# Attend pass of a Performer and RWKV block: where TensorE takes the maxima of a group, and where VectorE reduces them

## The reference

```
def _phi(u, omega):                       # 16 heads of 32, 128 features
    proj = einsum('bhsk,mk->bhsm', u, omega)
    sq   = 0.5 * sum(u * u, axis=-1, keepdims=True)
    stab = max(proj, axis=-1, keepdims=True)
    return exp(proj - sq - stab) / sqrt(128) + 1e-06

pq, pk = _phi(q * scale, omega), _phi(k * scale, omega)
kv, z  = einsum('bhsm,bhsk->bhmk', pk, v), sum(pk, axis=2)
num    = einsum('bhsm,bhmk->bhsk', pq, kv)
den    = einsum('bhsm,bhm->bhs', pq, z)
h      = (num / den) @ wo
y      = layernorm(xn + h)                # then feed-forward, gelu, a second layernorm

r   = sigmoid(xr @ W_r.T)                 # xr, xk: mixes of xn and xn of the token before
out = r * (square(relu(xk @ W_k.T)) @ W_v.T)
```

## Time and profile before

| | |
|---|---|
| median of 3 runs | 3194.19 us (3192.41 to 3194.93) |
| the profiled execution | 3190.72 us, span 3188.9 us |
| PE, weight loads | 3125.2 us (98%), 2770.3 us (87%) |
| DVE, ACT, POOL | 72%, 52%, 32% of the span |
| keys pass, attend pass, feed-forward pass | to about 760 us, to about 1790 us, to the end |
| granted TensorE clock, mean | 0.992 |

### The profile page before, as it was taken

The page is one execution under the profiler, slowest core; times in us unless marked ns, Lnnn a source line. Parts: engine busy times, 40 slices in busy tenths (PEclk is TensorE's granted clock), DMA queues, the critical chain, the costliest instruction groups (busy, mean ns, idle before and its releaser), DMA issues.

```text
span 3188.9 us, 71767 instructions
## 1 busy us (share of the span) xinstructions
PE 3125.2 (98%) x27633; PEld 2770.3 (87%) x27633; DVE 2290.8 (72%) x4582; ACT 1644.1 (52%) x3560; POOL 1028.1 (32%) x828
## 2 busy tenths in 40 slices
PE   8999999997999999999999999999999999999998
PEld 6888888886878787777777799999999999999998
DVE  6888888886666666666666666666766766767666
ACT  5677777764555454554555544444444444444443
POOL 2455544544555565565656310000000000000000
PEclk9999999998999999999999999999999999999999
DMA  7666666654354544444444665444445554444454
GB/s 227 202 188 194 201 187 200 197 189 101 90 156 115 144 126 131 125 134 123 138 135 117 201 218 171 157 163 158 152 161 166 167 171 159 160 165 148 160 169 133
DMA packets 450307, 510.17 MB, mean 160 GB/s; under 512 B 298800, under 2 KB 323888, under 8 KB 449968
## 3 DMA queue, kind: packets, MB, share of 16 engines
q1 hardware_dynamic: 449968, 505.59, 51.0%
HBM read 342.83 MB, written 162.66 MB: 159 GB/s over the span
## 4 chain that ended last, share of the span: by engine, by line
PE 55%; POOL 10%; DVE 3%; issue 3%; ACT 3%; DMA 2%; SPq 1%; ACTq 0%; DVEq 0%; POOLq 0%
PE ffn_hidden L188 29%; PE shared_bank L188 12%; PE ffn_result L188 7%; POOL shared_y L1209 3%; PE attend_feat L1372 2%; POOL shared_y L1207 2%; POOL attend_oT_lo L1191 2%; PE attend_num L1410 2%; PE attend_turn L1410 2%; POOL attend_ka_lo L1187 1%; POOL shared_mix_lo L1183 1%; DMA ffn_r_in<-r_d 1%; DVE ffn_yb L1834 1%; ACT attend_act_k L1252 1%; ACT attend_ka_hi L1256 1%
## 5 line engine op out<-in xcount | busy, mean ns | idle before, releaser
L188 PE MATMUL ffn_hidden<-ffn_yT_hi,ffn_wa_hi 128*128 128x256 f32 x2048 | 572.6, 280 | 2.5 <-DVE ffn_wa_lo L1755 2.5
L188 PE MATMUL ffn_hidden<-ffn_yT_lo,ffn_wa_hi 128*128 128x256 f32 x2048 | 573.6, 280 | 0.0
L188 PE MATMUL ffn_hidden<-ffn_yT_hi,ffn_wa_lo 128*128 128x256 f32 x2048 | 572.2, 279 | 0.0
L333 POOL TENSOR_TENSOR ffn_n_rstd<-ffn_n_base,ffn_n_power 128x2 f32<-128x2 f32 x32 | 27.5, 860 | 1274.7 <-DVE ffn_n_negmean L328 1274.7
L188 PEld LDWEIGHTS ffn_hidden<-ffn_yT_hi,ffn_wa_hi 128*128 128x128 f32 x2048 | 385.6, 188 | 3.4 <-DVE ffn_wa_lo L1755 2.7
L188 PEld LDWEIGHTS ffn_hidden<-ffn_yT_hi,ffn_wa_lo 128*128 128x128 f32 x2048 | 385.7, 188 | 0.0
L188 PEld LDWEIGHTS ffn_hidden<-ffn_yT_lo,ffn_wa_hi 128*128 128x128 f32 x2048 | 385.3, 188 | 0.2
L1737 ACT ACTIVATE ffn_ht_hi<-ffn_hs 128x512 fp32r<-128x512 f32 x248 | 156.3, 630 | 426.0 <-DVE ffn_hs L1784 426.0
L728 ACT ACTIVATE keys_e<-keys_feat,keys_below 128x128 f32<-128x128 f32 x1024 | 273.0, 436 | 187.0 <-DVE keys_below L811 187.0
L655 POOL TENSOR_TENSOR keys_z_sum<-keys_z_sum,keys_e 128x512 f32<-128x512 f32 x192 | 262.5, 1397 | 257.0 <-ACT keys_e L728 257.0
L1788 DVE TENSOR_TENSOR ffn_ht_lo<-ffn_hs,ffn_ht_hi 128x512 fp32r<-128x512 f32 x248 | 173.7, 700 | 218.7 <-ACT ffn_ht_hi L1737 218.7
(11 more groups left out here) (306 smaller groups left out, 9218.2 us busy)
## 6 DMA issues: line engine op xcount, KB each, us to landing
ffn_tq<-part_d SPq DMA_DIRECT2D x248, 512.0 KB, 5.1
keys_xin<-in_L_attn_x_dram SPq DMA_DIRECT2D x32, 512.0 KB, 4.3
xn_d<-keys_xn SPq DMA_DIRECT2D x32, 512.0 KB, 5.2
xt_d<-keys_xn_turned SPq DMA_DIRECT2D x32, 512.0 KB, 2.7
keys_xT_whole<-xt_d SPq DMA_DIRECT2D x128, 128.0 KB, 3.2
xT_d<-keys_xT_whole SPq DMA_DIRECT2D x32, 512.0 KB, 3.9
kt_d<-keys_uk_turned SPq DMA_DIRECT2D x32, 512.0 KB, 3.5
keys_kT<-kt_d SPq DMA_DIRECT2D x128, 128.0 KB, 3.4
```

The source lines that it names most:

```text
L188: last = pe.matmul(out, stationary[a], moving[b], start=start and n == 0, stop=stop and n == len(TERMS) - 1)
```

## The change

On PE, `max` 0 moves from behind the four `num` blocks to ahead of them, and `max` 1 from between `k` 0 and `k` 1 to ahead of `k` 0. A turn is then `max` 0, `num` 0 to 3, `max` 1, `k` 0, `k` 1 and the rest as it was. On DVE, `top` 0 leaves the start of the list and is done for the next group at its end, between `wo` 1 and `stats`; `HEAD` gets `top` 0 of the first group, ahead of `mix` 1. The lists of the crossing follow. No instruction is added or taken away.

```diff
--- before.py
+++ after.py
@@ -1061,12 +1061,12 @@
 
 
 
-        PE_BODY = [("num", 0, -1), ("num", 1, -1), ("num", 2, -1), ("num", 3, -1), ("max", 0, 0), ("k", 0, 0),
-                   ("max", 1, 0), ("k", 1, 0), ("r", 0, 0), ("below", 0, 0), ("feat", 0, 0), ("r", 1, 0), ("out", 0, 0),
+        PE_BODY = [("max", 0, 0), ("num", 0, -1), ("num", 1, -1), ("num", 2, -1), ("num", 3, -1), ("max", 1, 0),
+                   ("k", 0, 0), ("k", 1, 0), ("r", 0, 0), ("below", 0, 0), ("feat", 0, 0), ("r", 1, 0), ("out", 0, 0),
                    ("feat", 1, 0), ("out", 1, 0), ("wo", 0, -1), ("wo", 1, -1)]
-        DVE_BODY = [("top", 0, 0), ("top", 1, 0), ("recip", 0, -1), ("below", 0, 0), ("mix", 0, 1), ("exp", 0, 0),
+        DVE_BODY = [("top", 1, 0), ("recip", 0, -1), ("below", 0, 0), ("mix", 0, 1), ("exp", 0, 0),
                     ("o", 0, -1), ("out", 0, 0), ("turn_y", 0, -2), ("hi", 1, 0), ("out", 1, 0), ("mix", 1, 1), ("wo", 0, -1),
-                    ("wo", 1, -1), ("stats", 0, -1), ("part_lo", 0, 0)]
+                    ("wo", 1, -1), ("top", 0, 1), ("stats", 0, -1), ("part_lo", 0, 0)]
         ACT_BODY = [("num", 0, -1), ("num", 1, -1), ("num", 2, -1), ("num", 3, -1), ("norm", 0, -2), ("k", 0, 0),
                     ("k", 1, 0), ("below", 0, 0), ("kv", 0, 0), ("r", 0, 0), ("exp", 0, 0), ("mix", 0, 1), ("r", 1, 0),
                     ("oT", 0, -1), ("exp", 1, 0), ("mix", 1, 1), ("part_hi", 0, 0)]
@@ -1077,7 +1077,7 @@
                    ("rep_load", 0, -1), ("store_y", 0, -2), ("xb", 0, -1), ("store_r", 0, 0), ("store_yT", 0, -2),
                    ("kv", 0, 0),
                    ("part_load", 0, 0), ("part_store", 0, 0)]
-        HEAD = [("mix", 1)]
+        HEAD = [("top", 0), ("mix", 1)]
         OF_BATCH = {"kv": 0, "part_load": 0, "part_sums": 0, "part_hi": 1, "part_lo": 2, "part_store": 3}
 
         def run(eng, do, order):
@@ -1917,8 +1917,8 @@
         return Programs(sync, gpsimd, scalar, vector, tensor, mem), y_loaded, stored
 
 
-PE_CROSSING = (("attend", "num", 0, -2), ("attend", "num", 1, -2), ("attend", "num", 2, -2), ("attend", "num", 3, -2),
-               ("attend", "max", 0, -1), ("attend", "k", 0, -1), ("attend", "max", 1, -1), ("attend", "k", 1, -1),
+PE_CROSSING = (("attend", "max", 0, -1), ("attend", "num", 0, -2), ("attend", "num", 1, -2), ("attend", "num", 2, -2),
+               ("attend", "num", 3, -2), ("attend", "max", 1, -1), ("attend", "k", 0, -1), ("attend", "k", 1, -1),
                ("attend", "r", 0, -1), ("attend", "below", 0, -1), ("attend", "feat", 0, -1), ("attend", "r", 1, -1),
                ("attend", "out", 0, -1), ("attend", "feat", 1, -1), ("attend", "out", 1, -1), ("attend", "wo", 0, -2),
                ("attend", "wo", 1, -2), ("attend", "num", 0, -1), ("attend", "num", 1, -1), ("attend", "num", 2, -1),
@@ -1928,7 +1928,7 @@
                ("ffn", "w2", 2, 0), ("ffn", "w2", 3, 0), ("ffn", "w1", 5, 0), ("ffn", "w2", 4, 0),
                ("ffn", "w1", 6, 0), ("ffn", "w1", 7, 0), ("ffn", "w2", 5, 0),
                ("ffn", "w2", 6, 0), ("ffn", "w2", 7, 0))
-DVE_CROSSING = (("attend", "top", 0, -1), ("attend", "top", 1, -1), ("attend", "recip", 0, -2),
+DVE_CROSSING = (("attend", "top", 1, -1), ("attend", "recip", 0, -2),
                 ("attend", "below", 0, -1), ("attend", "exp", 0, -1), ("attend", "o", 0, -2),
                 ("attend", "out", 0, -1), ("attend", "turn_y", 0, -3), ("attend", "hi", 1, -1), ("attend", "out", 1, -1), ("attend", "wo", 0, -2),
                 ("ffn", "weights", 0, 0), ("attend", "wo", 1, -2), ("ffn", "turn", 0, 0), ("attend", "stats", 0, -2),
```

## The result

| | before | changed |
|---|---|---|
| median, 7 runs each | 3194.19 us (3191.12 to 3198.28) | 3204.24 us (3201.84 to 3206.89) |
| ratio to before | | 1.0031 (1.0021 to 1.0041) |
| span of the profiled execution | 3188.9 us | 3200.0 us |
| PE busy, DVE busy | 3125.2, 2290.8 us | 3121.6, 2368.4 us |

The changed kernel is 0.3% slower, 10 us. The direction and the place were as forecast (3215), but the size was not: +21 us were forecast, and +10 came. PE's busy time is hardly changed. DVE's is 78 us longer although it does the same work.

What follows compares the result with a forecast made beforehand. Two paths bound the attend pass: PE from `wo` 0 to the end of `k` 1, and POOL from the second `ka_lo` on. Terms 0 + 1 + 14 + 5 + 1 = +21 us on 3194.2 gave 3215 us, range 3195 to 3236.

Steps and rivals of the forecast that it cites:

- The statistics are 2.8 us late: On DVE in the attend pass, the statistics wait behind `top` 0 and begin 2.8 us later, delaying POOL.
- The room in turns without `part_sums`: On POOL, 3.2 us of room absorbs 2.8 in 22 groups; seven with `part_lo` lose 1 us together.
- The turn behind `part_sums`, +2.0 us: On POOL, seven groups with `part_sums` each lose 2.0 us (1.5 to 2.8), 14 us in all.
- The lateness of the second `ka_lo`: On POOL in groups with `part_sums`, the second `ka_lo` starts behind the first and ends 0.7 us later.
- The 0.1 for the small steps beside `part_sums`: DVE's three small `below` steps, now beside POOL's `part_sums`, add 0.1 us (0 to 0.3) per such group.
- the price of a `mix` piece: Each of DVE's four `mix` 0 pieces between POOL instructions costs POOL 0.3 us (0.20 to 0.42), +1.2 together.
- The clock, +5 us: PE's longer wait before `wo` dips the granted clock in 3 of 7 groups: 5 us (0 to 11).
- PE's shape changes, 0: On PE, 0.18 us saved per group is offset by `max` 0 to `num` 0: net 0 (-2 to +7).
- a period below 32.2: Sign of a wrong forecast: turns under 32.2 us would mean shape changes were dearer before than read.
- Start and crossing, +1: At the attend pass's start and crossing, delays and a shorter first wait together cost +1 us (-3 to +5).
- Rival 3: Worse: DVE's `o` waits for POOL's `mix_lo` 0 and every such group loses its clock; +41, 3235 us; chance 0.16.
- rival 1: Lateness mostly absorbed: DVE's pieces slip in for nearly nothing, the clock holds; +7, 3201 us; chance 0.24.

Runs made afterwards that it cites:

- e1: The changed kernel with DVE's statistics put ahead of the next group's first maxima again, PE's new order kept: 3202.17 us, 1.0023 of before.
- e2: The changed kernel with PE's part undone and DVE's part kept, so the statistics wait for later maxima: 3321.25 us, 1.0400 of before.
- e3: The changed kernel with POOL's `part_sums` run one turn later, behind `oT_lo`, where POOL is idle: 3192.23 us, 0.9999 of before.
- e9: The changed kernel itself measured once more, with no further edit: 3202.26 us, 1.0031 of before.
- e5: The kernel before the change with one exchange on POOL, `oT` ahead of `mix` 0: 3179.86 us, 0.9962 of before.

## Why the prediction was wrong in its size

Point by point, with the term that it used and what the runs showed:

- **The statistics are 2.8 us late: right.** POOL's root starts 5.60 us into the turn instead of 2.86. e1 takes the lateness away and the long turns go with it, e2 makes it 6.4 and both `ka_lo` start within 0.15 us of where they were worked out.
- **The room in turns without `part_sums`: right, and better than thought.** 1 us was set aside for the turns with `part_lo`; they lose nothing (32.25 against 32.23 for their neighbour).
- **The turn behind `part_sums`, +2.0 us: too dear.** Measured +1.45. PE's 0.18 has no part in it, because this turn's path doesn't pass through the `k` blocks. The lateness of the second `ka_lo` was right: it starts 15.21 into the turn on average, at 1456.2 in the turn shown, where the forecast's own steps (all times in it moved to this turn) give 1456.1. The 0.1 for the small steps beside `part_sums` was right too: from the first `part_sums` to `diff` POOL takes 3.23 us instead of 3.13. The step that failed is the price of a `mix` piece. Taken at 0.3 us between 0.20 and 0.42, it costs POOL 0.19 three times and 0.07 once: four make 0.63, not 1.2. The row of before (0.20) had shown nearly that, and I moved away from it towards a bound that no row showed. e3 shows where the term comes from: with `part_sums` moved, 1.65 us go from each of the seven turns.
- **The clock, +5 us: wrong, and the largest miss.** The granted clock didn't fall in any of the seven long turns. PE's wait rose to 1.9 us and not to 2.5, because the term above was too large. The step that failed is the comparison with the crossing. The forecast set one wait of 2.5 us against a dip, but its own rows show two waits there, 2.7 and 2.5 us, with PE busy for only 6.20 of the ten us before the dip. A long turn has one wait, and PE is busy for 8.55 of ten. In e2, where PE stands several times in a turn, the clock falls in each of the seven.
- **PE's shape changes, 0: wrong by 4 us the other way.** The loss was bounded by the opposite order, `num` to `max` with 0.41 us of idle loads, and the gain by 0.10. By the forecast's own sum the bound of 0.10 gives -0.08 in a turn. Measured is -0.18: the 0.18 that leaves the `k` blocks was read rightly, and `max` 0 ahead of `num` 0 costs nothing more. So the gain lies outside the stated -2 to +7 us. The forecast had named a period below 32.2 as a sign that it had misread the changes, and the fourth kind of turn has 32.18. By the Trainium skill's rule that a change of tiling mode drains TensorE (TensorEngine Tiling (Array Packing), section Tiling Modes) and one change fewer, the forecast had -3 us beside its own 0, and that was nearer. The equal price that this count takes for all changes isn't what the rows show: from the last matmul of one block to the first of the next, the change from column to row tiles takes 0.31 us, and those from row tiles to column tiles and to whole ones 0.21.
- **Start and crossing, +1: too cheap.** The start gave +0.5 in the profiled execution, but the second execution of the changed kernel (e9) has its second turn at 820.41, 1.2 us earlier than before, so no loss is shown there. Three of the forecast's parts can be seen: the wait for ACT's first copy shrank from 2.6 to 1.2 us, the stretch at half clock behind it (790.1 to 793.5 before) is gone, and PE waits 3.3 us for `mix_lo` where it waited 0.3, 3.0 us more, where up to 2.4 was allowed for `mix` 1 behind `top` 0. The crossing has the wait that was named there, 3.2 us and not at most 2.3, since `recip` waits for its DMA longer than it did before and `below` stands behind it. The profiled stretch is 4 to 6 us longer than before, and the wait alone costs some 4 us by the estimate above, so most of it arrives.
- **The rivals.** Rival 3's point of decision was read right: `o` came 0.15 us ahead of `mix_lo`, against 0.2 worked out, and so the worse case didn't come. The measured 3204 lies nearer to rival 1 (3201) than to the forecast: its clock, which holds, came true, and its pieces that cost nearly nothing didn't.

Sum of the terms, forecast and measured in the profiled span: PE's order 0 and -3.8; turns with `part_lo` 1 and 0 (in the line before); turns behind `part_sums` 14 and +10.2; clock 5 and 0; start and crossing 1 and +4.7. Together 21 and 11. The mechanism of the loss was right and its sizes were not: the clock and the long turns were too high, the gain in the other turns was set at nothing, and only the crossing was too low. That the crossing cost 3.7 us more than forecast is luck for the total, since it hides part of the other misses.

## What to carry to other kernels

Of a step that moves ahead of another on one engine, follow the second one's result to the engine that waits for it, and add up that engine's whole queue up to the point where the critical path enters it: room that is there in three turns of four isn't room. Price an interleaving by the row that shows it, not by a worse bound that no row shows, and give a gain its term as well as a loss. Where one engine's unbroken run ends just after the bound engine asks, look at the order within that run first: here one exchange of two POOL steps was worth more than all else.

## What the runs showed of the hardware

- Some DVE instructions and POOL's instructions take turns when both wait. DVE pays with a whole POOL instruction each time (1.67 us of work took 5.78), POOL with 0.07 to 0.19 us for a piece of 0.48 (0.40 from start to start). Those held here are `mix`, `below` and `o`, which read two SBUF tensors, and also the cast at L1312, which reads one: 1.22 us instead of 0.23. The maxima, read from PSUM, ran beside POOL at their full speed (2.49 us).
- From the last matmul of one block to the first of the next, the change from row tiles to column tiles takes as long as that from row tiles to whole ones (0.21 us), while the change from column to row tiles takes 0.31 us and leaves the weight loads idle for 0.41. A block of maxima between the two `k` blocks costs 0.18 us more than one between `wo` and `num`.
- Idle time of the weight loads of 0.55 us ahead of `wo` was worth 0.38 us of time (e5).
- A single stop of PE of 1.9 us (weight loads) was followed by full clock in seven turns of seven in the changed kernel. In e2, stops of 0.6, 1.1 and three times 0.3 us were followed by 3.4 or 6.8 us at half clock in seven of seven.
